# A mega-kernel's schedule table: output projection in four uses of bank 7, row preparation respread over the slots

## The chip, the cores and the metric

The kernel runs on one core of a Trainium2 chip. The metric is the device time of one execution in microseconds, median of several runs; the engines are TensorE (PE; its weight loads are PEld), VectorE (DVE), ScalarE (ACT), GpSimd (POOL) and SyncE (SP), which issues the DMAs.

## The reference

A layer with hyperbolic (Poincare) attention of 16 heads of width 16 over 8 sequences of 1024 tokens, and an FFN with one FP8-quantised product. Cut to what matters:

```python
x = x + attn(layernorm(x));  x = x + ffn(layernorm(x))
# attn, per head, c = softplus(log_c):
q_h, k_h, v_h = (exp_map_at_origin(split_heads(x @ W.T), c) for W in (W_q, W_k, W_v))
dist = poincare_distance(q_h, k_h, c)                 # arccosh(1 + 2c|q-k|^2 / ((1-c|q|^2)(1-c|k|^2)))
weights = softmax(-beta_pos * dist - attention_bias)
out_tan = einsum('bhst,bhtd->bhsd', weights, log_map_at_origin(v_h, c))
out = log_map_at_origin(exp_map_at_origin(out_tan, c), c)   -> concat @ W_o.T
# ffn: y = (e4m3(x / s_in) @ e4m3(kernel / s_k)) * (s_in * s_k), bf16, + bias
```

The exponential map needs a norm of each head's vector (an inverse square root, made here by a guess and three Newton steps on VectorE) and a tanh (made from one small exponential on ScalarE).

## The kernel before

The main loop has N = 512 steps: 16 stages (STEPS = 32 slots each) of 512 query tokens; in a stage, four groups of four heads, and for each group eight tiles of 128 keys. A slot s of stage G is one tile: distances of four heads by TensorE (`distances`, L1100, 18 x 128 weights on 512 columns, into banks 0 to 5), a logarithm of 128 x 2048 (`log`, L1217) and a power (`power`, L1224) by ScalarE, and the weighted values (`values`, L1115, summed in bank 6). The distances of slot n + 1 need the banks that the logarithm of slot n has read. In a unit of four slots whose flag says "open", VectorE bounds and clamps first (`bound` L1285, `clamp` L1294) and ScalarE reads its result (L1212); here three units of 128 are open: slots 4 to 7 of stage 5, 20 to 23 of stage 8, 12 to 15 of stage 15.

Beside this loop run the stages before and after the attention, all through the one bank 7, in *uses*: TensorE fills the bank, VectorE copies it out, and the next use waits for that copy. `project_stage` makes q, k, v of block n: X0 and X1 (transposes of the normalised input), M0 to M7 (the projections), R0 to R7 (transposes of the scaled rows of q and k), A0 and A1 (their largest entries, for the flags). `finish_stage` ends block n: T0, T1 (transposes), W (output projection, L695, and the residual, L723), Q0, Y0, Y1 (the FFN). S0 to S3 turn the sums of a head group (slots 2, 10, 18, 26; `turn_sums` L1124, `normalise` L1308 to L1312). The order is written out by hand: PROJECT_USES, FINISH_USES, FIRST_USES (project 1) and SECOND_USES (project 2) name slot and half for each use. From project 3 on, table slot k lies in slot k - 4 of stage n - 2; the finish of block n has k = slot in stage n + 1. BOTH means that the first half of the use goes ahead of the slot's values on TensorE and the second half behind them; a use with half 0 or 1 is done whole there. Slots without a use get two filler matmuls (`keep_busy`, L1138), except the slot BARE.

The functions `vector` of both stages hold VectorE's other work by table slot k: squares and sums (L587, L588), guess and Newton steps (L261 to L269), nrm (L596), the scaling of v (L598 to L604), the tanh and the row entries (L610 to L629), and `scale_rows` (L554). ScalarE's small exponential (`scalar`, L529) waits for nrm. In each slot VectorE first makes the copies of that slot's uses, in order (`copy`), then `copy_sums`, then the finish's and the project's other work. Before a unit of four slots each engine waits for a flag, loads it and branches. `Steps` makes VectorE wait for an own result where the next instruction reads it: a call waits, `mark` doesn't. In stage 15 SHORT_SLOTS says which table slots of the finish of block 14 fall into which slot. Ahead of the loop, project 0 and most of project 1 are done in many banks (FIRST_FILLS), and behind it comes the finish of block 15 (`last_tensor`, `last_vector`) with fillers at L1142.

## Time and profile before

| | |
|---|---|
| median of 3 runs | 1991.97 us (1991.16 to 1992.04) |
| the profiled execution | 1994.49 us, span 1992.7 us |
| mean granted TensorE clock | 0.972 of full speed |
| ScalarE busy | 1869.9 us, 94% |
| TensorE busy | 1788.6 us, 90% |
| VectorE busy | 1142.9 us, 57% |
| loop | first logarithm at 47.3, last power over at 1955.9 us |

A row of the trace gives start, duration, engine, line, operation, output and inputs and, in brackets, how long the engine was idle before and what released it. Consecutive instructions of one line stand in one row (x8: eight records, two for each fp32 matmul). Durations overlap a little on one engine, so the pitch from start to start is what counts. "DVEq" is VectorE's sequencer; "issue" is idle time for which the profile shows no wait.

### The profile page before, as it was taken

How to read it: one execution, taken by the hardware profiler on the slowest of the kernel's cores; microseconds unless marked ns; L12 is line 12 of the kernel's file. 1: busy time of each engine (PE TensorE's matmuls, PEld its weight loads, DVE VectorE, ACT ScalarE, POOL GpSimd, SP SyncE). 2: the span in 40 equal slices, each digit the busy share in tenths (PEclk: the TensorE clock that was granted, in tenths of full speed). 3: DMA queues.
4: the chain of work that ended last, by engine and by line, in shares of the span. 5: the costliest groups of instructions: out<-in, count | busy, mean ns of one | idle time of the engine just before them, and what ended most of it. 6: DMA issues, size and time to landing. Idle time of an engine off the chain costs nothing.

```text
span 1992.7 us, 29554 instructions
## 1 busy us (share of the span) xinstructions
PE 1788.6 (90%) x10713; PEld 603.1 (30%) x10713; DVE 1142.9 (57%) x2825; ACT 1869.9 (94%) x1094; POOL 12.8 (1%) x35
## 2 busy tenths in 40 slices
PE   7988989989898798989998898998989899899897
PEld 4322222323232232322322223232322223233234
DVE  7454565655656656565656647565565656323436
ACT  4889999999999799999998999999999999999883
POOL 2000000000000000000000000000000000000000
PEclk9799999999999899999999899999999999999889
DMA  1314213141312213132040321314131131411110
GB/s 56 112 49 144 54 54 103 42 134 43 112 44 78 77 44 112 43 101 75 23 134 22 110 67 44 112 43 134 40 107 52 56 90 43 123 43 53 33 33 23
DMA packets 112953, 142.54 MB, mean 72 GB/s; under 512 B 35691, under 2 KB 61548, under 8 KB 112748
## 3 DMA queue, kind: packets, MB, share of 16 engines
q1 hardware_dynamic: 112748, 140.13, 22.6%
q8 instruction: 89, 1.46, 0.3%
q14 instruction: 116, 0.95, 0.2%
HBM read 85.07 MB, written 55.05 MB: 70 GB/s over the span
## 4 chain that ended last, share of the span: by engine, by line
ACT 54%; PE 24%; issue 14%; DVE 4%; ACTq 3%; DMA 0%; DVEq 0%; SPq 0%
ACT U L1217 28%; ACT U L1224 26%; PE ps L1100 8%; PE ps L401 6%; PE ps L1115 5%; ACTq L1265 2%; PE ps L695 2%; DVE U L1294 1%; PE ps L1138 1%; PE ps L406 1%; PE ps L1142 1%; DVE U L1285 1%; DVE rows L554 0%; DMA U<-in_L_attn_W_o_dram 0%; ACT e L529 0%
## 5 line engine op out<-in xcount | busy, mean ns | idle before, releaser
L1224 ACT ACTIVATE U<-U 128x2048 f32<-128x2048 f32 x512 | 997.1, 1949 | 0.3
L1217 ACT ACTIVATE U<-ps 128x2048 f32<-128x2048 f32 x500 | 955.7, 1911 | 35.5 <-PE ps L1100 31.6
L1100 PE MATMUL ps<-q_T,k_T 18*128 18x512 f32 x4096 | 632.5, 652 | 133.0 <-ACT U L1217 107.7
L1115 PE MATMUL ps<-U,vals 128*32 128x512 f32 x4096 | 560.4, 620 | 29.4 <-ACT U L1224 28.9
L1100 PEld LDWEIGHTS ps<-q_T,k_T 18*128 18x128 f32 x4096 | 195.9, 187 | 356.8 <-ACT U L1217 296.4
L401 PE MATMUL ps<-wT,xnT 128*128 128x384 f32 x512 | 232.0, 545 | 4.9 <-DVEq L1318 2.5
L490 DVE COPY qkv<-ps 128x384 f32<-128x384 f32 x112 | 62.4, 557 | 243.7 <-PE ps L401 243.6
L1115 PEld LDWEIGHTS ps<-U,vals 128*32 128x32 f32 x4096 | 81.7, 109 | 205.4 <-ACT U L1224 159.2
L401 PEld LDWEIGHTS ps<-wT,xnT 128*128 128x128 f32 x512 | 81.1, 194 | 197.0 <-issue 132.4
L1138 PE MATMUL ps<-woT,ident 128*128 128x256 f32 x340 | 121.8, 441 | 3.8 <-DVEq L1318 3.6
L406 PE MATMUL ps<-ident,rows 128*128 128x128 f32 x512 | 107.2, 308 | 4.9 <-DVE rows L554 2.4
L406 PEld LDWEIGHTS ps<-ident,rows 128*128 128x128 f32 x512 | 55.1, 146 | 176.4 <-issue 114.5
L1138 PEld LDWEIGHTS ps<-woT,ident 128*128 128x128 f32 x340 | 52.0, 193 | 145.2 <-issue 116.0
L1300 DVE COPY OTs<-ps 128x512 f32<-128x512 f32 x64 | 43.8, 684 | 88.0 <-PE ps L1115 75.3
L498 DVE COPY q_T<-ps 128x512 f32<-128x512 f32 x60 | 41.5, 691 | 90.9 <-PE ps L406 90.3
L500 DVE COPY k_T<-ps 128x512 f32<-128x512 f32 x60 | 41.5, 691 | 62.8 <-PE ps L406 60.8
L695 PE MATMUL ps<-woT,fi_ocT 128*128 128x256 f32 x240 | 68.6, 409 | 0.0
L1308 DVE TENSOR_REDUCE den<-ps 128x16 f32<-128x256 f32 x64 | 27.2, 424 | 58.2 <-PE ps L1124 57.2
L695 PEld LDWEIGHTS ps<-woT,fi_ocT 128*128 128x128 f32 x240 | 41.0, 191 | 51.8 <-issue 37.3
L723 DVE TENSOR_TENSOR fi_x<-fi_xt,ps 128x512 f32<-128x512 f32 x30 | 20.6, 688 | 61.9 <-PE ps L695 61.9
L587 DVE TENSOR_TENSOR sqr<-qkv 128x768 f32<-128x768 f32 x56 | 53.3, 953 | 2.4
L588 DVE TENSOR_REDUCE ss<-sqr 128x48 f32<-128x768 f32 x56 | 53.4, 953 | 1.9
(209 smaller groups left out, 1179.6 us busy)
## 6 DMA issues: line engine op xcount, KB each, us to landing
rqb<-q_scratch SPq DMA_DIRECT2D x64, 1024.0 KB, 5.6
q_scratch<-q_T SPq DMA_DIRECT2D x16, 1024.0 KB, 4.5
k_scratch<-k_T SPq DMA_DIRECT2D x16, 1024.0 KB, 6.8
v_scratch<-vals SPq DMA_DIRECT2D x16, 768.0 KB, 9.6
...
```

What stands on the lines that cost most here:

```text
L401: ins = pe.matmul(bank[:, 0:384], xnT[:, dc, t * P:(t + 1) * P], g.wT[:, dc, half * 384:(half + 1) * 384], start=dc == 0, stop=dc == 1)
L406: ins = pe.transpose(bank[:, t * P:(t + 1) * P], rows[:, qk, t, hg * HPG:(hg + 1) * HPG, :].rearrange("p h r -> p (h r)"), g.ident[:, :])
L490: v.tensor_copy(qkv[:, t, 24 * half:24 * (half + 1), :].rearrange("p h d -> p (h d)"), bank[:, 0:384]).then_inc(a.b7_copied, 1)
L587: step(v.tensor_tensor(sqr[:, :], src, src, ALU.mult))
L588: step(v.tensor_reduce(ss[:, t, :], sqr[:, :].rearrange("p (h d) -> p h d", d=DH), AX.X, ALU.add))
L695: ins = pe.matmul(bank[:, a * D:(a + 1) * D], ocT[:, dc, t * P:(t + 1) * P], g.woT[:, dc, :], start=dc == 0, stop=dc == 1)
L1100: ins = pe.matmul(g.ps[:, 2 * pair + i, :], a.k_T[HB * h:HB * h + RD, b % 2, hg, kt * P:(kt + 1) * P], a.q_T[HB * h:HB * h + RD, G % 3, hg ...
L1115: ins = pe.matmul(g.ps[HB * h:HB * h + VW, 6, :], a.vals[:, b % 2, kt, (hg * HPG + h) // 2, DH * (h % 2):DH * (h % 2) + VW], U[:, n % RING ...
L1138: pe.matmul(g.ps[:, 7, 0:D], g.ident[:, :], g.woT[:, 0, :], start=True, stop=True)
L1217: act.activation(U[:, n % RING].rearrange("p b n -> p (b n)"), chunk(n), ACT.Ln, scale=-2.0 / EPS, bias=1.0).then_inc(freed, 1)
L1224: act.activation(U[:, n % RING], U[:, n % RING], ACT.Exp, scale=exponent).then_inc(exp_done, 1)
L1300: v.tensor_copy(OTs[:, :], g.ps[:, 6, :]).then_inc(ot_done, 1)
```

## The change

The tables: W becomes four uses (W0 to W3 in table slots 15, 16, 17, 19), each of one token tile with its bn_stats in the same slot; M3 goes from table slot 10 to 11; A0 from 27 to 24 (second half, alone in its slot); R2 is a use of both halves; the bare slot is 6. Project 2's and project 1's uses are moved likewise. VectorE's work: squares of tiles 1 and 2 from table slots 11 and 14 to 12 and 15, two Newton steps in slot 18 and one with nrm in 19, the scaling of v from 20 to 35, the tanh spread over 21 to 23, amax ahead of the second reciprocal, the row entries and the scaling of q's rows together in 24 (behind A0's copy), that of k's rows in 25. The small exponential moves from table slot 21 to 20, which is slot 16. The four stores go from 34 to 36. The finish has its first scaling in 7, the aggregates in 20, the last sum in 33. Stage 15 packs the finish of block 14 into earlier slots, and the tail has 19 fillers for 24. The rest of the diff renames slots accordingly.

```diff
@@ -47,32 +47,35 @@
...
-PROJECT_SLOTS = 35
-FINISH_SLOTS = 34
+PROJECT_SLOTS = 37
+FINISH_SLOTS = 35
 PROJECT_USES = {("X", 0): (4, BOTH), ("X", 1): (5, BOTH),
-                ("M", 0): (7, BOTH), ("M", 1): (8, BOTH), ("M", 2): (9, BOTH), ("M", 3): (10, BOTH),
+                ("M", 0): (7, BOTH), ("M", 1): (8, BOTH), ("M", 2): (9, BOTH), ("M", 3): (11, BOTH),
                 ("M", 4): (12, BOTH), ("M", 5): (13, BOTH), ("M", 6): (15, BOTH), ("M", 7): (16, BOTH),
-                ("R", 0): (25, BOTH), ("R", 1): (26, BOTH), ("R", 2): (27, 0), ("A", 0): (27, 1),
+                ("A", 0): (24, 1), ("R", 0): (25, BOTH), ("R", 1): (26, BOTH), ("R", 2): (27, BOTH),
                 ("R", 3): (28, BOTH), ("R", 4): (29, BOTH), ("R", 5): (31, 0), ("A", 1): (31, 1),
                 ("R", 6): (32, BOTH), ("R", 7): (33, BOTH)}
 TOLD = 12
-FINISH_USES = {("T", 0): (13, BOTH), ("T", 1): (14, BOTH), ("W", 0): (15, BOTH), ("W", 1): (17, BOTH),
+FINISH_USES = {("T", 0): (13, BOTH), ("T", 1): (14, BOTH), ("W", 0): (15, BOTH), ("W", 1): (16, BOTH),
+               ("W", 2): (17, BOTH), ("W", 3): (19, BOTH),
                ("Q", 0): (30, BOTH), ("Y", 0): (31, 0), ("Y", 1): (31, 1)}
-
-SHORT_USES = dict(FINISH_USES)
-SHORT_USES.update({("Q", 0): (28, BOTH), ("Y", 0): (30, 0), ("Y", 1): (30, 1)})
-BARE = 7
-SHORT_SLOTS = {23: (23, 24), 24: (25, 26), 25: (27, 28), 26: (29,), 27: (30, 31), 28: (32,), 29: (33,), 30: (), 31: ()}
+BARE = (6,)
+
+SHORT_SLOTS = {8: (8, 9, 10, 11, 12), 9: (13,), 10: (), 11: (14,), 12: (15,), 13: (16,), 14: (17, 18), 15: (19,), 16: (20, 21),
+               17: (22,),
+               18: (23,), 19: (24,), 20: (25,), 21: (26, 27), 22: (28, 29, 30), 23: (31, 32), 24: (33,), 25: (34,),
+               26: (), 27: (), 28: (), 29: (), 30: (), 31: ()}
 SUM_STEPS = 10
 
 
 FIRST_USES = {("A", 0): (2, 0), ("R", 4): (2, 0), ("A", 1): (2, 0), ("R", 5): (3, BOTH), ("R", 6): (6, BOTH),
-              ("R", 7): (11, BOTH), ("R", 0): (14, BOTH), ("R", 1): (17, BOTH), ("R", 2): (19, BOTH),
-              ("R", 3): (20, BOTH)}
+              ("R", 7): (14, BOTH), ("R", 0): (17, BOTH), ("R", 1): (19, BOTH), ("R", 2): (20, BOTH),
+              ("R", 3): (21, BOTH)}
 
 SECOND_USES = dict(PROJECT_USES)
-SECOND_USES.update({("R", 0): (25, BOTH), ("R", 1): (26, BOTH), ("R", 2): (27, 0), ("A", 0): (27, 1), ("R", 3): (28, 0),
-                    ("R", 4): (28, 1), ("R", 5): (29, BOTH), ("R", 6): (30, 0), ("A", 1): (30, 1), ("R", 7): (31, BOTH)})
+SECOND_USES.update({("M", 2): (9, BOTH), ("M", 3): (11, BOTH),
+                    ("R", 0): (25, BOTH), ("R", 1): (27, 0), ("R", 2): (27, 1), ("R", 3): (28, 0), ("R", 4): (28, 1),
+                    ("R", 5): (29, BOTH), ("R", 6): (30, 0), ("A", 1): (30, 1), ("R", 7): (31, BOTH)})
 
 FIRST_FILLS = ([("X", 0, 0, 6), ("X", 0, 1, 7)] + [("M", 0, i, (2, 3, 4, 5, 6, 7, 2, 3)[i]) for i in range(8)]
...
+    OWN = {0: 9, 1: 10, 9: 2, 12: 2, 15: 2, 17: 3, 18: 7, 19: 3, 21: 2, 22: 4, 23: 5, 24: 4}
     PER = sum(OWN.values())
 
...
+        if k == 36:
             b, u = n // 2, n % 2
...
+                pe.wait_ge(rows_rdy, 2 * n + (1 + i // HG if n >= 2 else 2 - i // HG))
         ins = fill(pe, n, key, g.ps[:, 7, :], part)
         if part != 0:
...
 
     def scalar(act, n, k):
-        if k == 21:
+        if k == 20:
             act.wait_ge(n_rdy, n + 1)
...
             ins.then_inc(xn_rdy, 1)
-        if k in (9, 11, 14, 17):
-            t = {9: 0, 11: 1, 14: 2, 17: 3}[k]
+        if k in (9, 12, 15, 17):
+            t = {9: 0, 12: 1, 15: 2, 17: 3}[k]
             v.wait_ge(a.b7_copied, uses.after(("M", n, 2 * t + 1)))
...
             root_guess(v, step, ss[:, :, :], y[:, :, :])
+            newton(v, step, ss[:, :, :], y[:, :, :], y2[:, :, :], 2)
+        if k == 19:
             newton(v, step, ss[:, :, :], y[:, :, :], y2[:, :, :], 1)
-        if k == 19:
-            newton(v, step, ss[:, :, :], y[:, :, :], y2[:, :, :], 2)
             v.tensor_tensor(nrm[:, :, :], ssqk, yqk, ALU.mult).then_inc(n_rdy, 1)
-        if k == 20:
+        if k == (31 if n == 2 else 35):
+            step = first or Steps(v, g_steps, 2 * (n - 2))
             step(v.tensor_scalar(vg[:, :, :], y[:, :, 2 * H:], g.ZS, 1.0, ALU.mult, ALU.min))
...
             step(v.reciprocal(rp[:, :, :], rp[:, :, :]))
+        if k == 22:
             step.mark(v.tensor_scalar(tn[:, :, :], e[:, :, :], -1.0, 1.0, ALU.mult, ALU.add))
             step(v.tensor_tensor(a4[:, :, :], e[:, :, :], rp[:, :, :], ALU.mult))
             step.mark(v.tensor_tensor(tn[:, :, :], tn[:, :, :], rp[:, :, :], ALU.mult))
             step(v.tensor_tensor(a4[:, :, :], a4[:, :, :], rp[:, :, :], ALU.mult))
-        if k == 22:
+        if k == 23:
+            step.mark(v.tensor_scalar(a4[:, :, :], a4[:, :, :], 4.0, A_FLOOR, ALU.mult, ALU.max))
             step.mark(v.tensor_tensor(tt[:, :, :], tn[:, :, :], tn[:, :, :], ALU.mult))
             step.mark(v.tensor_tensor(f[:, :, 0:H], tn[:, :, 0:H], yqk[:, :, 0:H], ALU.mult))
-            step.mark(v.scalar_tensor_tensor(f[:, :, H:], tn[:, :, H:], 2.0, yqk[:, :, H:], ALU.mult, ALU.mult))
-            step(v.tensor_scalar(a4[:, :, :], a4[:, :, :], 4.0, A_FLOOR, ALU.mult, ALU.max))
+            step(v.scalar_tensor_tensor(f[:, :, H:], tn[:, :, H:], 2.0, yqk[:, :, H:], ALU.mult, ALU.mult))
+            v.tensor_reduce(amax[:, :], a4[:, :, :].rearrange("p t h -> p h t"), AX.X, ALU.max).then_inc(amax_rdy, 1)
             step(v.reciprocal(rp[:, :, :], a4[:, :, :]))
-        if k == 23:
+        if k == 24:
             if n >= 4:
                 v.wait_ge(a.stored, 64 * n)
             step.mark(v.tensor_copy(rows[:, 0, :, :, 17], tt[:, :, 0:H]))
             step.mark(v.tensor_copy(rows[:, 0, :, :, 18], rp[:, :, 0:H]))
             step.mark(v.tensor_copy(a.rk[:, b % 2, :, u * GT:(u + 1) * GT], rp[:, :, H:].rearrange("p t h -> p h t")))
             step.mark(v.tensor_scalar(rows[:, 1, :, :, 16], tt[:, :, H:], -1.0, None, ALU.mult))
-            v.tensor_reduce(amax[:, :], a4[:, :, :].rearrange("p t h -> p h t"), AX.X, ALU.max).then_inc(amax_rdy, 1)
-        if k == 24:
-            scale_rows(v, n, (1, 0))
-        assert first or step.n == OWN.get(k, 0), (k, step.n)
+            if n >= 2:
+                scale_rows(v, n, (0,))
+        if k == 25:
+            scale_rows(v, n, (1,))
...
-                sp.wait_ge(steps_v, PER * (n - 1) + sum(count for slot, count in OWN.items() if slot <= 28))
+                sp.wait_ge(steps_v, PER * (n - 1) + sum(count for slot, count in OWN.items() if slot <= 27))
             sp.dma_start(xt[:, :, :], g.x_g[n]).then_inc(f_in, 16)
-        if k == 33:
+        if k == 34:
             sp.wait_ge(res_rdy, n + 1)
...
-            for a in halves(part, range(2)):
-                t = 2 * i + a
-                for dc in range(2):
-                    ins = pe.matmul(bank[:, a * D:(a + 1) * D], ocT[:, dc, t * P:(t + 1) * P],
-                                    g.woT[:, dc, :], start=dc == 0, stop=dc == 1)
+            for dc in halves(part, range(2)):
+                ins = pe.matmul(bank[:, 0:D], ocT[:, dc, i * P:(i + 1) * P], g.woT[:, dc, :],
+                                start=dc == 0, stop=dc == 1)
         elif kind == "Q":
...
                     v.wait_ge(res_out, 16 * n)
-            v.tensor_tensor(x1[:, two, :].rearrange("p t d -> p (t d)"),
-                            xt[:, two, :].rearrange("p t d -> p (t d)"), bank, ALU.add).then_inc(b7_copied, 1)
+            v.tensor_tensor(x1[:, i, :], xt[:, i, :], bank[:, 0:D], ALU.add).then_inc(b7_copied, 1)
         elif kind == "Q":
...
                             y[:, :, :].rearrange("p t h -> p (t h)").unsqueeze(2).broadcast_to([P, GT * H, DH]),
                             ALU.mult).then_inc(oc_rdy, 1)
-        if k == 21:
-            v.wait_ge(b7_copied, uses.after(("W", n, 1)))
-            for t in range(GT):
-                step.mark(v.bn_stats(stats[:, t, :], x1[:, t, :]))
+        if k in (15, 16, 17, 19):
+            t = {15: 0, 16: 1, 17: 2, 19: 3}[k]
+            v.wait_ge(b7_copied, uses.after(("W", n, t)))
+            step.mark(v.bn_stats(stats[:, t, :], x1[:, t, :]))
+        if k == 20:
             step.settle()
...
         if k == 26:
             v.tensor_tensor(xq[:, :, :].rearrange("p t d -> p (t d)"), sp2, sp1, ALU.subtract).then_inc(xq_rdy, 1)
-        if k == 28:
+        if k == 27:
             step(v.tensor_reduce(rmax[:, :], xt[:, :, :], AX.X, ALU.max, apply_absolute_value=True))
...
         pe.wait_ge(l_act, 2)
-        keep_busy(1, 24)
+        keep_busy(1, 19)
...
                         use(*key, 0)
-                    unused = n > 2 and s != BARE and not in_step(G, s, 0) + in_step(G, s, 1)
+                    unused = n > 2 and s not in BARE and not in_step(G, s, 0) + in_step(G, s, 1)
```

## Rows read from the trace of the kernel before

**Rows 1.** The page's first section, and one row of the waits.

```profile
PE 1788.6 (90%) x10713; PEld 603.1 (30%) x10713; DVE 1142.9 (57%) x2825; ACT 1869.9 (94%) x1094; POOL 12.8 (1%) x35
...
ACT U L1217 <- PE ps L1100: 31.6, 21, 5.9
```

**Rows 2.** Timeline of ScalarE, stage 9, slots 16 to 20 (start, duration).

```profile
1192.16 1.88 ACT L1217 ACTIVATE U<-ps 128x2048 f32<-128x2048 f32 x1
...
1195.99 1.88 ACT L1217 ACTIVATE U<-ps 128x2048 f32<-128x2048 f32 x1
...
1199.56 0.39 ACT L529 ACTIVATE e<-nrm,sc 128x128 f32<-128x128 f32 x1
1199.85 1.87 ACT L1217 ACTIVATE U<-ps 128x2048 f32<-128x2048 f32 x1
...
1207.07 1.87 ACT L1217 ACTIVATE U<-ps 128x2048 f32<-128x2048 f32 x1
```

**Rows 3.** Timeline of TensorE, stage 9: slot 15, and slot 21's first transpose.

```profile
1190.52 1.24 PE L1100 MATMUL ps<-q_T,k_T 18*128 18x512 f32 x8 [0.33 <-ACT U L1217]
1191.69 1.13 PE L695 MATMUL ps<-woT,fi_ocT 128*128 128x256 f32 x4
1192.75 1.07 PE L1115 MATMUL ps<-U,vals 128*32 128x512 f32 x8
1193.75 1.13 PE L695 MATMUL ps<-woT,fi_ocT 128*128 128x256 f32 x4
...
1213.73 0.44 PE L406 MATMUL ps<-ident,rows 128*128 128x128 f32 x2
```

**Rows 4.** Timeline of VectorE, stage 9, slots 15 to 20.

```profile
1197.54 0.36 DVE L269 SCALAR_TENSOR_TENSOR y<-y 128x192 f32<-128x192 f32 x1
1197.93 0.29 DVE L596 TENSOR_TENSOR nrm<-ss,y 128x128 f32<-128x128 f32 x1
1199.34 0.69 DVE L1300 COPY OTs<-ps 128x512 f32<-128x512 f32 x1 [1.12 <-issue]
...
1207.71 0.95 DVE L621 RECIPROCAL rp<-a 128x128 f32<-128x128 f32 x1
...
1209.14 0.37 DVE L629 TENSOR_REDUCE amax<-a 128x32 f32<-128x128 f32 x1
1210.04 2.36 DVE L554 TENSOR_TENSOR rows<-qkv,f 128x1024 f32<-128x1024 f32 x2 [0.53 <-issue]
```

**Rows 5.** VectorE's groups by form: count, busy, mean ns, idle before.

```profile
L752 DVE BATCH_NORM_STATS2 fi_stats<-fi_x 128x6 f32<-128x256 f32 x60 | 20.9, 412 | 2.7 <-issue 2.7
...
L502 DVE TENSOR_REDUCE amax_r<-ps 32x1 f32<-32x128 f32 x16 | 4.5, 278 | 8.6 <-PE ps L411 8.6
...
L886 DVE TENSOR_TENSOR fi_x<-fi_xt,ps 128x256 f32<-128x256 f32 x4 | 1.7, 417 | 0.7 <-PE ps L842 0.7
```

**Rows 6.** First stage: ScalarE and TensorE rows; then stretches (length, busy, PEclk last but two).

```profile
109.50 1.88 ACT L1217 ACTIVATE U<-ps 128x2048 f32<-128x2048 f32 x1 [5.93 <-PE ps L1100]
...
68.09 2.09 PE L1100 MATMUL ps<-q_T,k_T 18*128 18x512 f32 x8
...
73.22 2.09 PE L1100 MATMUL ps<-q_T,k_T 18*128 18x512 f32 x8
...
165.75 0.44 PE L406 MATMUL ps<-ident,rows 128*128 128x128 f32 x2 [1.72 <-DVEq L1318]
...
160.00:166.70 6.70, 4.38 (x34) 1.65 (x34) 2.65 (x7) 6.66 (x4) 0.00 (x0) 1.00 0.01 0
166.70:173.50 6.80, 6.80 (x35) 2.02 (x31) 1.46 (x3) 3.78 (x3) 0.00 (x0) 0.50 0.01 2
```

**Rows 7.** Timeline of ScalarE, stage 8, slot 20: first logarithm of the open unit.

```profile
1085.72 1.91 ACT L1212 ACTIVATE U<-U 128x2048 f32<-128x2048 f32 x1 [4.65 <-DVE U L1294]
```

**Rows 8.** The tail: TensorE's fillers, and VectorE's last step ahead of the transposes.

```profile
1969.26 10.63 PE L1142 MATMUL ps<-woT,ident 128*128 128x256 f32 x48
...
1977.67 1.23 DVE L903 TENSOR_TENSOR fi_xq<-fi_ocT,fi_osq 128x1024 bf16<-128x1024 f32 x1
```

45 lines of the change are left out of this document (20 added, 25 removed).

## Prediction

> **What bounds the kernel now.** I read the shares first: ScalarE is busy for 94% of the span, TensorE for 90%, VectorE for 57% [rows 1]. The waits of ScalarE before its logarithm come second: 31.6 us of idle time behind the distances, in only 21 places [rows 1]. So the rhythm is ScalarE's, one logarithm and one power per slot, and time is lost in a few places. Third comes the timeline of a regular stage, stage 9. I count from the start of the logarithm of slot 16, at 1192.16. A logarithm starts 3.57 us before the place where the next could start: slot 17's at 1195.99, and its successor's place is taken at 1199.56 by the small exponential, which pushes the next logarithm to 1199.85, 0.29 later [rows 2]. I use 3.56 for a full ScalarE slot. From slot 16 to slot 20 the logarithms need 1207.07 - 1192.16 = 14.91 instead of 14.24, so 0.67 is lost per stage: 0.29 to the small exponential, 0.38 to the doubled output projection in slots 15 and 17, which makes TensorE late [rows 2, 3]. What slots 5 to 8 lose to the projections of q, k, v stays (below).
>
> TensorE's order in a slot is fixed: distances (first at 1.92 after its logarithm), first half of a use, the values as soon as the power is over, second half [rows 3]. VectorE runs its own program in order: a copy out of bank 7 waits for the second half, and all that stands behind that copy waits too.
>
> **Part 1, the output projection in four uses, and the exponential in slot 16.** A whole use is now one quarter: a half takes 0.53 instead of 1.06 [rows 3]. TensorE is no longer late in slots 15 to 19 and 0.38 goes. But in slot 15 VectorE must copy the first quarter, do bn_stats, three Newton steps and the product nrm, and the small exponential in slot 16 waits for nrm. Slot 15 starts at 1188.60 (1192.16 less 3.56): distances at 1190.52, values at 3.72, so at 1192.3, second half from 1193.31, filled at 1193.9, copied from 1194.0, that is 1.86 after slot 16's logarithm. Then 0.42 for a copy of 256 columns plus 0.04, 0.33 for bn_stats (four take 1.4, mean 0.41, overlapping) [rows 5], 3 x 0.39, and 0.29 for nrm [rows 4]: 4.11. The exponential starts at 4.15 instead of 3.56, the next logarithm at 4.44. Slots 16 to 20 then take 4.44 + 3 x 3.56 = 15.12, against 14.91: **+0.21 per stage**, x 13 stages = +2.7. In stage 14, without projections, only the 0.38 is gained: -0.4. What hid nrm before was a whole slot between it and the exponential.
>
> **Part 2, rows and A0.** This is the part that decides. Before, slot 19 had no use of bank 7, VectorE ran ahead, and both scalings of the rows started at 1210.04, 2.97 after slot 20's logarithm at 1207.07, and were over at 5.33; the first transpose R0 was due at 1213.73, that is 6.66 [rows 2, 3, 4]. Now slot 19 holds the last quarter (W3) and slot 20 holds A0, and the whole chain stands behind them. From slot 20's logarithm: W3 is copied from 1.85 (as above) to 2.31; bn_stats to 2.64; the four small products before the reciprocal at 1207.71, 0.73 as there; amax 0.28 (its 0.37 less the overlap); the reciprocal 0.95 and its wait: 4.64 [rows 4]. Slot 20 begins a unit of four, where the sequencer waits for that reciprocal, reads the flag and branches: the same gap was 1.12 of issue at 1199.34 [rows 4], I take 1.05: 5.7. A0's reduction 0.28 [rows 5] and two semaphores: 6.15. The aggregates that the finish stage now has in slot 20, 0.6: 6.75. The four copies, 0.44 up to 1209.14, and the wait for the stores: 7.25. The q scaling, half of 2.36 [rows 4]: **rows ready at 8.5, due at 6.66**. TensorE stands for 1.85 us, with the values queued behind R0. R0's halves and the values take 0.37 + 0.99 + 0.37, so the next distances come at 10.3 instead of 9.05, and the logarithm of slot 23 at 11.46 instead of 10.68: +0.78 even if nothing else happens.
>
> The clock is what else happens. In the first stage TensorE stood 1.72 before a row transpose (165.75); over 160 to 166.7 it was busy 4.38 of 6.70, and from 166.7 to 173.5 the granted clock was 0.50, the 1.2 GHz level; ScalarE was then busy only 3.78 of 6.80 [rows 6]. The new gap of 1.85 follows a slot with no fillers (A0 replaces both), with gaps of 0.5 on each side of its values. Between 5.05 and 8.5 TensorE would work 1.24, less than in the case above. I expect the fall in nearly each stage. At the low level a slot with a row transpose takes 73.22 - 68.09 = 5.13 [rows 6] instead of 3.56; two such slots, the second logarithm about 2.1 after its distances begin, put slot 24's logarithm at 10.3 + 5.13 + 2.1 = 17.5 instead of 14.24: **+3.3**. Bounds: 1.8 if the clock comes back within a slot, 4.5 by the first stage's case with its stall (1.72 + 3.0 of ScalarE idle, rounded). It meets stages 1 to 13 except 8, where slots 20 to 23 are an open unit: 12 x 3.3 = +40 (22 to 54).
>
> The Trainium skill's page "TensorE: Matmul & The Clock Gate", section "HAM oscillation — how this bites in real kernels", ties the fall to waits long enough to cross an idle stretch, longer than this gap. By that rule the clock would hold here and 12 x 0.78 would be all (rival A). This case's trace disagrees with so mild a reading: it fell after a gap of 1.72 [rows 6].
>
> **Part 3, the open unit of stage 8.** Its first logarithm waited 4.65 us for VectorE's clamp [rows 7]. VectorE enters the unit after slot 19's work: before at about 17.9 after slot 16's logarithm (1210.04 - 1192.16), now at 15.12 + 5.7 = 20.8: +2.9.
>
> **Part 4, first stage.** M3 leaves the slot of the sums, where its wait ended in 5.93 us of idle ScalarE [rows 6], and R1 leaves slot 26, worth about 4. Against it: the squares of tile 1, two long instructions, now stand ahead of the quantising of the FFN kernel in slot 12, so M5's copy and R7 behind it come over 2 us late, a gap of the kind that cost 5.93; and slot 25 waits 1.2 for its rows. Between -10 and +2; I take -5.
>
> **Part 5, last stage and tail.** The finish of stage 14 runs up to four slots earlier. That empties slots 25 to 29, but puts T1's copy ahead of the open unit at slots 12 to 15 (+3.7 by the same count as part 3) and quarters into it. I take +0.8, between -5 and +6. In the tail five of 24 fillers go. They run from 1969.26 for 10.63, VectorE delivers xq at 1978.90 [rows 8], so at most 0.9 is open, and copies that wait for other work follow: -0.3.
>
> **At nothing**, each with its cover: M3 one slot later and the bare slot 6 for 7 (three projections in a row each side of the bare slot instead of four and two: the same lateness by the count of matmuls, an estimate); squares two slots later (VectorE idles there); Newton steps in slot 14 (2.4 us before the first quarter is filled, 0.4 to spare); v scaling to slot 31 (1.9 us, behind Y1's copy, 0.6 to spare); the four stores two slots later on SP's queue, whose first reader loads them a stage later.
>
> **The sum**, against the profiled execution (1994.49, its span 1992.7 and 1.8 around it): +2.7 - 0.4 + 40 + 2.9 - 5 + 0.8 - 0.3 = +40.7, so 2035.2. The median of the runs shown is 2.5 lower: **2033**. With 22 to 54 for part 2 and +-6 for the rest the forecast's own range is 2010 to 2052.
>
> **Rivals.** A, the rows are late but the clock holds: 12 x 0.78 = 9.4 instead of 40: 2002. For it: W3's and R0's matmuls lie around the gap. B, the change works: VectorE makes both appointments. The point is 4.8 us from W3's copy to the rows; I count 6.65. Then 13 x -0.38, -0.4, first stage -5, -0.3, no part 3: -10.6, that is 1981, faster. For it: VectorE has 43% idle, and my prices of semaphores and the branch could be too high, though hardly by 1.8. C, the gap of slot 16 (TensorE idle 1.06 while ScalarE waits for nrm) lowers the clock too: 13 x 2 more, 2059. D, it all cancels within 0.2%.
>
> **How the numbers follow.** About 0.2% (4 us) is what a measurement of this kernel can tell from no change. Forecast 0.60, A 0.17, B 0.12, C 0.07, D 0.04. Slower: 0.60 + 0.17 + 0.07 = 0.84, less a little of A: 0.83; faster 0.11; same 0.06. The range leaves out B and half of C: 1999 to 2056.
>
> **What would show it.** In the changed profile: L529's exponential in slot 16 with about 0.6 idle before it, released by nrm; the first row transpose of slots 21 with 1.5 to 2 us idle, released by the scaling of the rows, in each of stages 1 to 13; the granted clock at 0.5 for some slots behind it, mean clock well under 0.972; slots 15 to 19 without a late distance. If R0 starts without a gap, part 2 is wrong and the time is near 1981; if the gap is there and the clock stays 1.0, it is near 2002.

## The result and the profile after

The changed kernel takes 2038.51 us (median of 6 runs, 2036.11 to 2044.67) against 1992.01 for the kernel before (6 runs, 1991.16 to 1994.11): a ratio of 1.0235, 95% interval 1.0218 to 1.0252. The forecast was 2033, range 1999 to 2056. The profiled execution of after took 2036.56, its span is 2034.8, 42.1 more than before's, and its mean granted clock is 0.954 instead of 0.972. It lies 1.95 below the median of its kernel, where the forecast took 2.5 above; against the profiled execution the forecast was 2035.2.

First the page: the shares, and the groups of the logarithm and of the rows' transposes (busy, mean ns | idle before).

```profile
PE 1781.0 (88%) x10523; PEld 577.6 (28%) x10523; DVE 1145.2 (56%) x2855; ACT 1871.5 (92%) x1094; POOL 12.6 (1%) x35
...
L1218 ACT ACTIVATE U<-ps 128x2048 f32<-128x2048 f32 x500 | 954.9, 1910 | 60.0 <-PE ps L1101 57.5
...
L409 PE MATMUL ps<-ident,rows 128*128 128x128 f32 x512 | 117.9, 328 | 32.8 <-DVE rows L556 29.9
```

The engines have nearly the work of [rows 1]: VectorE is busy for 2.3 us more, ScalarE for 1.6 more, TensorE for 7.6 less. ScalarE waits 57.5 us for distances instead of 31.6, and TensorE waits 29.9 us for the scaling of the rows, where it waited 2.4 us in the kernel before. The two are one thing, as stage 9 shows. ScalarE there, from slot 16 (answers to [rows 2]):

```profile
1220.22 1.87 ACT L1218 ACTIVATE U<-ps 128x2048 f32<-128x2048 f32 x1
...
1224.46 0.40 ACT L532 ACTIVATE e<-nrm,sc 128x128 f32<-128x128 f32 x1 [0.56 <-DVE nrm L598]
1224.77 1.86 ACT L1218 ACTIVATE U<-ps 128x2048 f32<-128x2048 f32 x1
...
1235.44 1.88 ACT L1218 ACTIVATE U<-ps 128x2048 f32<-128x2048 f32 x1
...
1249.00 1.88 ACT L1218 ACTIVATE U<-ps 128x2048 f32<-128x2048 f32 x1 [2.75 <-PE ps L1101]
1250.77 1.90 ACT L1225 ACTIVATE U<-U 128x2048 f32<-128x2048 f32 x1
1253.33 1.88 ACT L1218 ACTIVATE U<-ps 128x2048 f32<-128x2048 f32 x1 [0.66 <-PE ps L1101]
```

The exponential waits 0.56 for nrm. The logarithms of slots 23 and 24 wait 2.75 and 0.66 for distances. TensorE in the same stage (answers to [rows 3]):

```profile
1226.68 1.24 PE L1101 MATMUL ps<-q_T,k_T 18*128 18x512 f32 x8 [1.03 <-ACT U L1218]
...
1239.17 1.07 PE L1116 MATMUL ps<-U,vals 128*32 128x512 f32 x8 [0.56 <-ACT U L1225]
1240.17 0.28 PE L414 MATMUL ps<-ident,amax 128*32 128x128 f32 x1
1240.94 1.24 PE L1101 MATMUL ps<-q_T,k_T 18*128 18x512 f32 x8 [0.48 <-ACT U L1218]
1244.59 0.41 PE L409 MATMUL ps<-ident,rows 128*128 128x128 f32 x2 [2.41 <-DVE rows L556]
...
1246.87 2.09 PE L1101 MATMUL ps<-q_T,k_T 18*128 18x512 f32 x8
```

TensorE stands 2.41 before R0, and the distances behind it take 2.09 instead of 1.24. VectorE is the releaser (answers to [rows 4]):

```profile
1237.41 0.42 DVE L727 TENSOR_TENSOR fi_x<-fi_xt,ps 128x256 f32<-128x256 f32 x1 [2.50 <-PE ps L699]
...
1239.21 0.94 DVE L626 RECIPROCAL rp<-a 128x128 f32<-128x128 f32 x1
1241.74 0.28 DVE L505 TENSOR_REDUCE amax_r<-ps 32x1 f32<-32x128 f32 x1 [1.58 <-issue]
1242.16 0.38 DVE L759 BATCH_NORM_AGGREGATE fi_mv<-fi_stats 128x2 f32<-128x6 f32 x4
...
1243.22 1.22 DVE L556 TENSOR_TENSOR rows<-qkv,f 128x1024 f32<-128x1024 f32 x1
```

W3's copy waits 2.50 for TensorE, then the chain runs through the unit's edge (1.58), A0's reduction, the aggregates and the copies. The clock, in stretches of one slot from 1241.58 (length, busy of PE, PEld, DVE, ACT, POOL, then PEclk):

```profile
1241.58:1245.14 3.56, 1.15 (x14) 0.36 (x10) 2.48 (x11) 3.56 (x3) 0.00 (x0) 1.00 0.52 194
1245.14:1248.70 3.56, 3.56 (x18) 0.81 (x10) 1.72 (x2) 1.11 (x1) 0.00 (x0) 0.55 0.42 103
1248.70:1252.26 3.56, 3.56 (x20) 1.04 (x20) 0.26 (x2) 3.26 (x2) 0.00 (x0) 0.50 0.02 5
```

TensorE is at its 1.2 GHz level for nearly two slots, full all the time, and in the first of them ScalarE is busy for 1.11 of 3.56 us. It is not so in every stage. Stage 11, the stretch behind such a gap, R0, and the logarithm of slot 23:

```profile
1483.00:1486.50 3.50, 3.50 (x28) 0.87 (x20) 1.82 (x2) 2.61 (x2) 0.00 (x0) 1.00 0.40 109
```
```profile
1482.49 0.41 PE L409 MATMUL ps<-ident,rows 128*128 128x128 f32 x2 [2.08 <-DVE rows L556]
...
1485.37 1.88 ACT L1218 ACTIVATE U<-ps 128x2048 f32<-128x2048 f32 x1 [0.89 <-PE ps L1101]
```

The clock held, and the whole stall costs 0.89 of idle ScalarE. Of the twelve regular stages (1 to 13 without 8) the clock held in two, 1 and 11, and fell in ten.

To put a number on each part I took the time from each logarithm to the next, less 3.56, and added it up by stage and slot. The excess goes to the later of the two slots. In all it is 84.0 us before and 126.6 after. The differences:

| part | before | after | difference |
|---|---|---|---|
| slots 16 to 19, stages 1 to 13 | 8.7 | 12.7 | +4.0 |
| slots 20 to 27, twelve regular stages | 0 | 41.5 | +41.5 |
| stage 8 from slot 20 on | 12.8 | 14.4 | +1.6 |
| stage 5, slots 0 to 15 | 16.0 | 18.5 | +2.5 |
| other slots 0 to 15, stages 1 to 13 | 6.9 | 6.5 | -0.5 |
| first stage | 24.0 | 21.0 | -3.0 |
| stage 14 | 0.8 | -0.1 | -0.9 |
| last stage | 14.9 | 12.2 | -2.7 |

### The profile page after: what moved, and what is told of

Read it like the earlier page. It is cut to its first block, busy times and chain, and to the rows that moved or that the text cites. A ratio compares the mean times of both kernels' runs of the same rounds, so it can differ in the third digit from the quotient of the medians.

```text
span 2034.8 us, 29206 instructions
## 1 busy us (share of the span) xinstructions
PE 1781.0 (88%) x10523; PEld 577.6 (28%) x10523; DVE 1145.2 (56%) x2855; ACT 1871.5 (92%) x1094; POOL 12.6 (1%) x35
## 4 chain that ended last, share of the span: by engine, by line
ACT 43%; PE 33%; issue 12%; DVE 9%; ACTq 2%; DVEq 1%; DMA 0%; SPq 0%
ACT U L1218 24%; ACT U L1225 19%; PE ps L1101 12%; PE ps L1116 9%; PE ps L404 8%; PE ps L409 2%; ACTq L1266 2%; PE ps L699 2%; DVE U L1295 1%; DVE rows L556 1%; DVE rp L626 1%; DVE U L1286 1%; DVE fi_x L727 1%; DVE fi_stats L755 1%; DVEq L1365 0%
## 5 line engine op out<-in xcount | busy, mean ns | idle before, releaser
L1218 ACT ACTIVATE U<-ps 128x2048 f32<-128x2048 f32 x500 | 954.9, 1910 | 60.0 <-PE ps L1101 57.5
L1225 ACT ACTIVATE U<-U 128x2048 f32<-128x2048 f32 x512 | 996.3, 1948 | 0.3
L1101 PE MATMUL ps<-q_T,k_T 18*128 18x512 f32 x4096 | 650.0, 666 | 162.8 <-ACT U L1218 124.9
L1116 PE MATMUL ps<-U,vals 128*32 128x512 f32 x4096 | 573.1, 633 | 32.5 <-ACT U L1225 31.6
L1101 PEld LDWEIGHTS ps<-q_T,k_T 18*128 18x128 f32 x4096 | 202.3, 191 | 390.3 <-ACT U L1218 322.5
L409 PE MATMUL ps<-ident,rows 128*128 128x128 f32 x512 | 117.9, 328 | 32.8 <-DVE rows L556 29.9
L409 PEld LDWEIGHTS ps<-ident,rows 128*128 128x128 f32 x512 | 57.5, 154 | 242.6 <-issue 183.2
L501 DVE COPY q_T<-ps 128x512 f32<-128x512 f32 x60 | 41.5, 691 | 114.1 <-PE ps L409 114.1
L727 DVE TENSOR_TENSOR fi_x<-fi_xt,ps 128x256 f32<-128x256 f32 x60 | 25.3, 421 | 116.6 <-PE ps L699 116.6
L699 PE MATMUL ps<-woT,fi_ocT 128*128 128x256 f32 x240 | 86.2, 441 | 0.0
L503 DVE COPY k_T<-ps 128x512 f32<-128x512 f32 x60 | 41.5, 692 | 50.5 <-PE ps L409 48.9
L699 PEld LDWEIGHTS ps<-woT,fi_ocT 128*128 128x128 f32 x240 | 36.7, 193 | 99.8 <-issue 77.0
L1213 ACT ACTIVATE U<-U 128x2048 f32<-128x2048 f32 x12 | 22.9, 1911 | 37.3 <-DVE U L1295 37.3
L1139 PE MATMUL ps<-woT,ident 128*128 128x256 f32 x160 | 56.2, 434 | 0.0
L721 DVE COPY fi_ocT<-ps 128x512 f32<-128x512 f32 x30 | 20.7, 692 | 57.4 <-PE ps L695 57.4
```

Of the source, the lines that this page charges most:

```text
L409: ins = pe.transpose(bank[:, t * P:(t + 1) * P], rows[:, qk, t, hg * HPG:(hg + 1) * HPG, :].rearrange("p h r -> p (h r)"), g.ident[:, :])
L699: ins = pe.matmul(bank[:, 0:D], ocT[:, dc, i * P:(i + 1) * P], g.woT[:, dc, :], start=dc == 0, stop=dc == 1)
L727: v.tensor_tensor(x1[:, i, :], xt[:, i, :], bank[:, 0:D], ALU.add).then_inc(b7_copied, 1)
L1101: ins = pe.matmul(g.ps[:, 2 * pair + i, :], a.k_T[HB * h:HB * h + RD, b % 2, hg, kt * P:(kt + 1) * P], a.q_T[HB * h:HB * h + RD, G % 3, hg ...
L1116: ins = pe.matmul(g.ps[HB * h:HB * h + VW, 6, :], a.vals[:, b % 2, kt, (hg * HPG + h) // 2, DH * (h % 2):DH * (h % 2) + VW], U[:, n % RING ...
L1139: pe.matmul(g.ps[:, 7, 0:D], g.ident[:, :], g.woT[:, 0, :], start=True, stop=True)
```

## The experiments

The theory: R0 comes late because VectorE's chain stands behind W3 and A0; the stall alone costs about 1 us a stage, and the fall of the clock that it brings costs two to three times as much again. Rivals: the clock only accompanies a loss that the wait makes; or A0, or W3, or the wait of slot 16 alone is the cause. Every kernel was timed beside the kernel before on the same chip, and ratios are to that. An expectation of so many us stands against 2038.5 for the change and 1992.0 for before, so 2011 is a ratio of 1.0096.

**The clock taken away, the wait kept.** In slot 21 of stages 1 to 13 TensorE gets fillers ahead of R0.

```diff
+                    if s == 21 and 1 <= G < LAST - 1:
+                        pe.wait_ge(a.b7_copied, first_use[n])
+                        keep_busy_again(7, 10)
                     for key in both:
                         use(*key, 0)
```

With ten:

> The changed kernel with ten fillers (128x256 matmuls whose result nobody reads) on TensorE in slot 21 of stages 1 to 13, behind the distances and ahead of the wait for the rows. They fill 10 x 0.22 of the 2.1 to 2.4 us in which TensorE stood; the rows come as late as before. My theory: the stall costs 1.02 a stage, as stages 1 and 11 of the changed kernel show, and the fall of the clock the rest, 2.84 to 4.47 in all in each of ten stages (39.5 together). With TensorE kept busy the clock holds in all twelve: 39.5 - 10 x 1.02 = 29.3 less, 2009. Rival, the clock is only a companion and the time is the stall's and VectorE's: no change or a little slower, 2038 to 2042. Second rival, the fall is prompted by something else in the slot (the DMA traffic, the light matmuls of A0): the clock still falls, 2038.

Measured: 1.0276 (1.0245 to 1.0306), so slower still. Stage 9:

```profile
1246.28 4.58 PE L1143 MATMUL ps<-woT,ident 128*128 128x256 f32 x20
1250.70 0.38 PE L409 MATMUL ps<-ident,rows 128*128 128x128 f32 x2
```

The number was missed for a plain reason, and the row shows it: ten fillers are x20 in the trace and take 4.58, so one is 0.46. I had read [rows 8] as 48 fillers in 10.63, where it is 24. TensorE was thus busy past the moment when the rows were ready, and R0 came at 11.11 after slot 20's logarithm. What the run did tell is clean: the clock held in all twelve stages at this place, and each was late by 3.25 to 3.33. With stage 11 of the change (R0 at 8.82, 1.02 late) this gives the point from which a late R0 costs, 7.8 after slot 20's logarithm, and behind it one us costs one us.

With five:

> As the kernel with ten fillers, but with five. In that kernel each filler took 0.46 us, not the 0.22 that I had counted (ten took 4.58), so that R0 came at 11.11 after slot 20's logarithm instead of 8.81 to 9.15, and slot 23's logarithm 3.27 late in every one of the twelve stages; the clock held in all twelve at the rows' place. The two place the point from which a late R0 costs anything at 11.11 - 3.27 = 7.84 and 8.81 - 1.02 = 7.79. Five fillers take 2.3, as long as TensorE stood. My theory: R0 starts when it did, at 8.8 to 9.15, each stage is 1.0 to 1.35 late, the clock holds: 2038.5 - 41.5 + 12 x 1.2 = 2011. Rival, what is lost is the stall's and the clock is a companion: 2036 to 2040.

Measured: 1.0119 (1.0088 to 1.0151), 2011.08 against the 2011 expected. The median of before was 1987.9 beside it, so the equal times are in part luck: by the ratio it lies 0.2% above the expected 1.0096, which is within the interval. Stage 9:

```profile
1229.15 0.41 PE L409 MATMUL ps<-ident,rows 128*128 128x128 f32 x2
...
1232.04 1.88 ACT L1221 ACTIVATE U<-ps 128x2048 f32<-128x2048 f32 x1 [1.21 <-PE ps L1101]
```

Nothing was made earlier here: 65 matmuls that nobody reads were added, and the rows are as late as in the change. Each regular stage is late by 1.11 to 1.39 (14.7 in all), the clock falls at this place in none, and half of the whole loss is gone. So the clock is a cause of its own and no companion. Of the 41.5 us some 12 to 15 are the stall and the rest, about twice that, is the clock.

**The wait made harmless.** R0 goes whole behind the values:

```diff
-                ("A", 0): (24, 1), ("R", 0): (25, BOTH), ("R", 1): (26, BOTH), ("R", 2): (27, BOTH),
+                ("A", 0): (24, 1), ("R", 0): (25, 1), ("R", 1): (26, BOTH), ("R", 2): (27, BOTH),
```

> The changed kernel with one appointment moved: R0, the first transpose of the rows, runs whole in the second half of slot 21, behind the values, instead of half before and half behind them. VectorE's chain is as it was and the rows are as late, 9.05 after slot 20's logarithm. My theory: the values (due at 7.28) no longer queue behind R0, the gap of 2.4 becomes 0.56 and about 0.9, R0 is over at 9.95 and the distances follow 0.9 late instead of 1.5, so slot 23's logarithm is late by about 0.45 instead of 1.02, and the clock holds: 2038.5 - 41.5 + 12 x 0.45 = 2002. If the clock falls in spite of the split gap: 2025 to 2035. Rival, only the moment when the rows are ready counts: no change, 2038.

Measured: 1.0051 (1.0031 to 1.0071), as expected (1.005). The same entry is changed for project 2. VectorE's chain is untouched. The values no longer queue behind R0:

```profile
1216.88 1.06 PE L1116 MATMUL ps<-U,vals 128*32 128x512 f32 x8 [0.56 <-ACT U L1225]
1218.73 0.63 PE L409 MATMUL ps<-ident,rows 128*128 128x128 f32 x4 [0.79 <-DVE rows L556]
```

The pause of 2.41 became 0.56 and 0.79, the clock fell at this place in none of twelve stages, and slot 23 is 0 to 0.25 late where 0.45 was expected. Slots 20 to 27 of the regular stages lose 1.0 instead of 41.5, so this one move gives back nearly all that part 2 lost. That the ratio hit all the same is luck: slots 16 to 19 lost 15.6 instead of 12.7, as the clock fell after the pause of slot 16 in three stages, and the first stage 16.0 instead of 21.0.

**Who makes the rows late.** A0 back in slot 23, in the half where it was:

```diff
-                ("A", 0): (24, 1), ("R", 0): (25, BOTH), ("R", 1): (26, BOTH), ("R", 2): (27, BOTH),
+                ("R", 0): (25, BOTH), ("R", 1): (26, BOTH), ("R", 2): (27, 0), ("A", 0): (27, 1),
```

> The changed kernel with A0, the transpose of the maxima, back in its old place in slot 23 (and R2 beside it); W3 stays in slot 19 and the rows are scaled as in the changed kernel. My theory: both W3 and A0 delay the rows. From slot 20's logarithm the reciprocal ends at 4.7, the pause at the unit's edge 1.1, then 2.3 for aggregates, copies and the scaling of q: rows at 8.1 instead of 9.05, R0 due at 6.74, so TensorE stands 1.35 instead of 2.1 to 2.4 and the logarithm of slot 23 is late by about 0.1 instead of 1.02. If the clock holds in all stages: 2038.5 - 41.5 + 1.2 = 1998. If it falls in half of them all the same: 2016. Rival, W3's copy is the cause and A0 costs nothing: the gap stays over 2 us, 2036 to 2039. Rival, A0 is the whole cause: no gap, 1997.

Measured: 1.0158 (1.0134 to 1.0181), nearest to the branch "falls in half of them" (2016), whose ratio of 1.012 lies outside the interval. W3 alone leaves R0 a pause of 1.65 in five stages and 1.94 to 2.03 in seven, where I had 1.35. Stage 6:

```profile
872.72 0.41 PE L409 MATMUL ps<-ident,rows 128*128 128x128 f32 x2 [1.66 <-DVE rows L556]
```

The clock held in all five stages with 1.65 and fell in five of the seven others. Slots 20 to 27 lose 23.0 instead of 41.5: W3 alone makes the rows late, and A0 adds 0.4 us to it.

W3 away from slot 19, to slot 18, with A0 left in slot 20; then with the exponential back too; then with A0 back as well:

```diff
-               ("W", 2): (17, BOTH), ("W", 3): (19, BOTH),
+               ("W", 2): (17, BOTH), ("W", 3): (18, BOTH),
```

> The changed kernel with W3, the last quarter of the output projection, in slot 18 beside the transpose of the sums, instead of in slot 19; A0 stays in slot 20 and the exponential in slot 16. (The last group has its quarters one slot apart to match.) My theory: VectorE is then 3.56 us earlier with the reciprocal, and A0 alone sets the rows: A0 filled at 5.0 after slot 20's logarithm, reduced by 5.3, then 2.4 for aggregates, copies and the scaling: R0 at about 8.0 to 8.2, 0.2 to 0.4 beyond the point where it costs. TensorE stands 1.4, and with A0 taken out the clock fell in none of the five stages whose gap was 1.65, in five of seven at 1.94 to 2.03. So no falls: 2038.5 - 41.5 + 3.6, and stage 8's open unit is entered 3.3 earlier, and slot 18 is 0.1 late 13 times: 1998.6. Rival, A0 is the cause and W3 is innocent: R0 as late as before, 2036. Rival, three uses of TensorE in slot 18 do not fit (1.24 + 0.66 + 1.4 + 1.07 = 4.4, less overlaps): 0.5 in each of 13 stages more, 2005.

> W3 in slot 18 and the small exponential in slot 17; A0 stays in slot 20. By my theory the two effects are separate and add: 1998.6 less 13 x 0.7 = 1989.5, a little under the kernel before. If the wait of slot 16 was hidden behind something else: 1998.

> The changed kernel with all three suspects undone: W3 in slot 18, the small exponential in slot 17, A0 in slot 23. The quarters of the output projection, the new places of M3 and of the first stage and the earlier finish of the last group stay. By my theory R0 of slot 21 starts without a gap, no clock falls there, the exponential costs 0.29 and slots 15 and 17 are not late: 2038.5 - 41.5 - 9.1 - 3.3 + 1.3 = 1986, 0.3% faster than the kernel before. If A0 in slot 23 makes slots 23 to 25 late as it did not in the kernel before, or the open unit of stage 8 stays late: 1990, no difference. A rival: W3 in slot 18 keeps VectorE so long that slot 18 to 20 run late: over 1995.

Measured: 1.0371 (1.0341 to 1.0402), 1.0356 (1.0315 to 1.0396) and 1.0270 (1.0244 to 1.0295). All three missed, and for one reason that none of my rivals named. Stage 9 of the first, TensorE and the end of VectorE's steps on the sums:

```profile
1245.49 0.66 PE L1125 MATMUL ps<-ident,OTs 128*128 128x128 f32 x4
1248.00 0.70 PE L699 MATMUL ps<-woT,fi_ocT 128*128 128x256 f32 x2 [1.84 <-DVEq L1319]
```
```profile
1247.40 0.49 DVE L1313 TENSOR_TENSOR on<-ps,den 128x128 f32<-128x128 f32 x2
```

Slot 18 turns the sums in bank 7, and bank 7 is free only when VectorE has taken them; W3's first half waits 1.84 for that, with the values behind it. I had counted TensorE's matmuls and not the bank's round trip through VectorE. In the third kernel the exponential's 0.29 and this pause (1.79) are all that is left in slots 16 to 27 of the regular stages: slot 20's logarithm is 1.87 late in the three stages where the clock held, 3.5 to 3.9 in the nine where it fell, and slot 21's up to 1.3 more. So they make the same pair of costs, a pause and a fall, in another slot and behind another step of VectorE. The second and the third differ by A0 and R2 alone, and with A0 in slot 20, W3 out of its way, R0 waits for the rows again. Stage 5 of the second:

```profile
758.58 0.41 PE L409 MATMUL ps<-ident,rows 128*128 128x128 f32 x2 [1.16 <-DVE rows L556]
```

This pause is 0.89 to 1.18 in its twelve regular stages, the clock fell at it in six of them, and slots 20 to 27 lose 69.1. With A0 back in slot 23 the pause is gone, and they lose 46.2. So A0 alone makes the rows late too.

**All undone that hurt, the rest kept.** The last two quarters share slot 17, one in each half, the exponential is in slot 17, A0 in slot 23:

```diff
-               ("W", 2): (17, BOTH), ("W", 3): (19, BOTH),
+               ("W", 2): (17, 0), ("W", 3): (17, 1),
...
-        if k == 20:
+        if k == 21:
             act.wait_ge(n_rdy, n + 1)
```

> The last two quarters of the output projection both in slot 17: W2 whole ahead of the values, W3 whole behind them. The small exponential is in slot 17, A0 in slot 23. With W3 in slot 18 TensorE stood 1.8 us in every stage, since the slot of the sums leaves no room for a second use of bank 7: the use waits for VectorE's four steps on the sums. In slot 17 nothing of that kind stands in the way. My theory: slot 17 has the matmuls that a doubled slot had before, 0.19 late (the doubled slot 15 is single now); the exponential costs 0.29; R0 of slot 21 has no gap, no clock falls in a regular stage, stage 8's open unit is entered as early as before. Per stage 0.48 instead of 0.67: -2.5; first stage -3 and last stage -2.6 as the changed kernel had them: 1984 against 1992 for the kernel before, a ratio of 0.996. Rival, the moved appointments of the first stage and of the last group gain only by the luck of the clock there: ratio 0.9985. Rival, W3's copy between W2's and the sums makes the sums late: over 1.00.

Measured: 0.9962 (0.9947 to 0.9977), where 0.996 was expected: faster than both kernels. The sum hit, its terms did not. In the profiled execution slots 16 to 19 lose 5.0 less than before (2.5 less expected), the first stage 6.7 less (3) and the last stage 3.9 less (2.6), while stage 5 loses 3.9 more and stage 14 3.6 more, which wasn't counted at all. R0 in slot 21 of stage 9 has no wait ahead of it:

```profile
1205.54 1.24 PE L1100 MATMUL ps<-q_T,k_T 18*128 18x512 f32 x8
1206.71 0.44 PE L409 MATMUL ps<-ident,rows 128*128 128x128 f32 x2
1207.34 1.07 PE L1115 MATMUL ps<-U,vals 128*32 128x512 f32 x8 [0.19 <-ACT U L1224]
```

The same with the FFN kernel's quantising in slot 10 of the first stage (`KERNEL_STEP = 10`):

> The same, and VectorE quantises the FFN kernel in slot 10 of the first stage, where its long steps stand behind the sums' and ahead of M3's copy, instead of in slot 12. In the changed kernel the pair of squares and these steps held M5's copy until 116.24, and R7 waited for it 2.36 us: slot 16's logarithm was 1.68 late. In slot 10 TensorE has no other use, M3's copy comes 1.2 late and M4's first half 0.7. My theory: 1.2 to 1.6 us less than with slot 12, a ratio lower by 0.0007; the clock of the first stage, which falls in other places in other runs, can move this by 3 us either way. Rival: nothing, because the stall moves to slot 11.

Measured: 0.9954 (0.9935 to 0.9973). R7's pause is gone; of slot 16's 1.67 us, 0.96 came back in slot 14. The two intervals overlap, so this gain isn't shown.

From the faster kernel each suspect was then put back alone. A0 in slot 20, with R2 in both halves as in the change:

> The kernel with W2 and W3 in slot 17 and the exponential in slot 17, but A0 in slot 20 as in the change: A0 alone. W3 no longer holds VectorE. My theory: A0 is filled at 5.0 after slot 20's logarithm, reduced by 5.3, and 2.3 to 2.4 more for the aggregates, the copies and the scaling of q: rows at 7.8 to 8.0, R0 0.1 to 0.3 beyond the point where it costs (7.8), TensorE stands 1.2 to 1.4, and the clock holds, as it did in all five stages with a gap of 1.65. 12 x 0.2 = 2.4 more: 0.9962 + 0.0012 = 0.9974. Rival, A0 was the whole cause and costs what it did in the changed kernel, 8.8 or more after slot 20's logarithm: 12 x 1.0 with the clock held, 1.002, or with falls up to 1.017.

Measured: 1.0069 (1.0042 to 1.0095), so +0.0107 where +0.0012 was expected. Stage 9, the reduction, then TensorE:

```profile
1227.56 0.28 DVE L505 TENSOR_REDUCE amax_r<-ps 32x1 f32<-32x128 f32 x1 [2.81 <-PE ps L414]
```
```profile
1227.24 0.29 PE L414 MATMUL ps<-ident,amax 128*32 128x128 f32 x1
1228.01 1.24 PE L1100 MATMUL ps<-q_T,k_T 18*128 18x512 f32 x8 [0.48 <-ACT U L1217]
1230.41 0.41 PE L409 MATMUL ps<-ident,rows 128*128 128x128 f32 x2 [1.16 <-DVE rows L556]
1230.75 1.93 PE L1115 MATMUL ps<-U,vals 128*32 128x512 f32 x8
```

The chain is as counted: R0 at 7.92 after slot 20's logarithm (1222.49), a pause of 1.16, and in the two stages where the clock held, 0.12 late. But the clock held in two stages only and fell in ten, with a shorter pause than the 1.65 that left it up five times. Ten may be more than is usual: the traced execution was the slowest of six, at a mean clock of 0.956 where the others had 0.958 to 0.967. In eight of the ten the clock fell before R0 started, by 0.03 to 0.65, that is inside the pause. The nearest difference between the two is slot 20: there fillers stood around the values, here A0's one matmul has their place and the pauses of 0.56 and 0.48 beside it. My expectation went by the length of the one pause and was wrong in that; that the thin slot 20 is the reason is argued and not shown. The kernel with R0 behind the values has the same thin slot 20 and pauses of 0.56 and 0.79, and never fell; what separates it from this one is not settled, and A0 in slot 20 with fillers beside it was not tried.

The exponential in slot 16:

> The kernel with W2 and W3 in slot 17 and A0 in slot 23, but the small exponential in slot 16 again: the one part alone, with no late rows behind it. My theory: 0.99 instead of 0.29 a stage as in the changed kernel, 13 x 0.70 = 9.1 more than the kernel with the exponential in slot 17: 0.9962 + 0.0046 = 1.0008 of the kernel before. Rival, TensorE's pause of 1.03 in slot 16 does lower the clock in some stages (the first trace of the exponential's removal could not exclude it, 10 falls of 12 against 9): 3 to 4 us for each, 1.003 or more. Rival, part of the wait lies under the doubled slot 17, so 0.5 a stage: 0.9995.

Measured: 1.0060 (1.0038 to 1.0082), +0.0098 where +0.0046 was expected. In the trace slot 17 is 0.99 late in each of 13 stages, as in the change, and slot 18 no longer 0.29; slot 19 loses 0.25 more, since the doubled slot 17 has no slack behind the pause; and in stages 5 and 13, where the clock fell after the pause of slot 16, slot 19 loses 1.84. Stage 5:

```profile
728.51 1.24 PE L1100 MATMUL ps<-q_T,k_T 18*128 18x512 f32 x8 [1.03 <-ACT U L1217]
729.68 1.83 PE L699 MATMUL ps<-woT,fi_ocT 128*128 128x256 f32 x4
```
```profile
730.00:733.40 3.40, 3.40 (x13) 0.97 (x11) 0.42 (x1) 3.40 (x3) 0.00 (x0) 0.50 0.00 0
```

Slots 16 to 19 of the 13 stages thus hold 19.2 instead of 3.7, that is 15.5 more for the 9.1 expected. In this execution the first and the last stage were 6.7 us longer besides and stage 14 4.0 shorter, which I can't tie to the edit.

The same part taken out of the change instead, with nothing else moved:

> The changed kernel with one part undone: the small exponential is back in slot 17 (the table's slot 21). Nothing else moves. My theory: in the changed kernel the logarithm of slot 17 comes 0.99 us late in each of 13 stages, 0.29 of it the exponential itself and the rest the wait for nrm and the pause that it leaves behind. Back in slot 17 the wait is hidden: 13 x 0.70 = 9.1 us less, 2029.4 against 2038.5. The rows of slot 21 stay as late as they were, and the clock still falls there. Rival 1, TensorE's pause of 1.03 us in slot 16 is what weakens it for the fall in slot 21: then falls in slot 21 vanish too, some 25 to 30 us more, about 2002. Rival 2, the 0.7 is taken from a slack that TensorE has later in the stage: no change, 2038.

Measured: 1.0152 (1.0131 to 1.0172), against 1.0188 expected. Slots 16 to 19 of the 13 stages fell from 12.7 to 3.7, which is the 9.0 expected. The rows' place lost 42.6 against 41.5, with nine falls instead of ten, so rival 1 (no falls left) is out. The median is 6.4 us below the profiled execution, which was the slowest of the four, at a clock of 0.950 where the others had 0.954 to 0.956: the part that the ratio gives beyond the 9.0 goes with that higher clock, but which falls were missing isn't known.

## Why the prediction was right

**The decisive step held: rows late, TensorE stands, the clock falls, in regular stages only.** The chain of part 2, counted from slot 20's logarithm at 1235.44: W3's copy at 1.97 (I had 1.85), the reciprocal over at 4.71 (4.64), A0's reduction over at 6.58 (6.15, as the edge took 1.58 where I took 1.05), rows ready at 9.00 (8.5), R0 at 9.15, pause 2.41 (1.85). The due time of 6.66 was 6.74. In the twelve regular stages the pause was 2.06 to 2.47, where the sign to look for was 1.5 to 2. Twelve times 3.3 made 40, the trace has 41.5. The runs with five fillers, with R0 behind the values and with the late uses moved away show each link of it.

**Two terms in it were off, and they cancel.** I had twelve falls at 3.3 each. There were ten, at 2.8 to 4.5, mean 3.95, and two stages at 1.0. The stall alone costs 1.0 (stages 1 and 11) to 1.39 (the run with five fillers), not 0.78, because the rows came at 8.7 to 9.1 instead of 8.5. So my certainty of a fall in each stage was too high and the price of one too low. My upper bound of 4.5 was set below the 4.7 that its own two numbers make, and the dearest stage took 4.47. All the other parts together were +0.7 by my count and +0.6 in the trace, though single ones missed by up to 3.5: that this sum came out is luck.

**Rival A was wrong in kind, not only in size.** By it the clock holds and 12 x 0.78 is all. The run with five fillers is that world made by hand. Rival A's 2002, with the stall at some 1.2 instead of 0.78, is 2007; measured were 2011, and by the ratio 2016. The Trainium skill's page "TensorE: Matmul & The Clock Gate", section "HAM oscillation — how this bites in real kernels", explains the fall by waits of some 3 to 5 us on a DMA between groups of matmuls. Here no single pause in the regular stages was longer than 2.47, the releaser was VectorE, and the clock fell in ten of twelve; the measurement decides. That section's picture, a fall paid again in each turn of the loop, is what the trace shows in ten of twelve stages.

**Rival C was half right.** The pause of 1.03 in slot 16 lowered the clock in none of 13 stages of the change, but in one to four of 13 in the other kernels that have it (A0 back 1, five fillers 1, R0 behind the values 3, ten fillers 4, the exponential put back into the faster kernel 2, W3 in slot 18 3). Each cost 0.9 to 1.0, 1.6 behind a doubled slot. Two us in each of 13 stages was far too much.

**Rival B, VectorE makes both appointments,** needed 4.8 us from W3's copy to the rows; it took 7.0 (1237.41 to 1244.44).

**Part 1.** The exponential started 4.24 after slot 16's logarithm (4.15 counted) and slots 16 to 20 took 15.22 (15.12). +4.0 instead of +2.7, 0.1 in each of 13 stages. Stage 14: -0.9 instead of -0.4.

**Part 3.** Stage 8's unit:

```profile
1115.44 1.91 ACT L1213 ACTIVATE U<-U 128x2048 f32<-128x2048 f32 x1 [7.95 <-DVE U L1295]
```

7.95 instead of 4.65 [rows 7], +3.3 for the 2.9 counted. The later slots of the unit gave half back, so +1.6 stayed. I had stopped at the first logarithm.

**Part 4.** -3.0 against -5. M3's 6.0 went, and R7's stall came where it was foretold, behind the quantising:

```profile
116.85 0.44 PE L409 MATMUL ps<-ident,rows 128*128 128x128 f32 x2 [2.36 <-DVE qkv L493]
```
```profile
119.76 1.88 ACT L1218 ACTIVATE U<-ps 128x2048 f32<-128x2048 f32 x1 [1.56 <-PE ps L1101]
```

The falls of the clock in slots 23 to 28 moved, but stayed. How much of the -3.0 the change made is open: with the same first stage, the traces with five fillers, with ten and with W3 in slot 18 have 17.7, 21.5 and 20.5 there, as the clock fell in other places.

**Part 5, the sign was wrong.** +0.8 counted, -2.7 measured. The step "puts T1's copy ahead of the open unit, +3.7" held:

```profile
1920.32 1.91 ACT L1213 ACTIVATE U<-U 128x2048 f32<-128x2048 f32 x1 [4.66 <-DVE U L1295]
```

It was 1.76 before, and the slot lost 7.0 instead of 3.7; slots 13 to 19 lose 2.6 more. The term that failed is what is emptied. Slots 27 to 29 gave 4.4, since the pause ahead of the last group's Q (2.09 in slot 26, with a fall behind it) is gone, and slots 9 to 11 gave another 4.1, which I had not counted at all. That second part is luck of the clock and no gain of the change. Before, the clock fell there behind two short pauses, and the change has the same two (0.56 and 0.70) without a fall:

```profile
1855.80 1.81 PE L1100 MATMUL ps<-q_T,k_T 18*128 18x512 f32 x8 [0.70 <-ACT U L1217]
...
1856.30:1866.60 10.30, 10.30 (x38) 2.43 (x30) 1.82 (x2) 7.58 (x5) 0.00 (x0) 0.50 0.01 2
```

With five fillers and in the two last kernels with W3 in slot 18 it fell there again. Without this 4.1 part 5 would be at +1.4, where I had counted +0.8. The tail gave 0.7 (0.3 counted, of at most 0.99 by [rows 8]).

**A step at nothing that wasn't.** The bare slot 6 for 7. In stage 5 the open unit ends with slot 7, at the low clock. Before, slot 7 had no projection and slot 8 began with TensorE idle for 0.97; now slot 7 has one, and slot 9's logarithm is 2.46 late (1.5 to 3.0 in the other kernels), +2.5 in all. My count of matmuls was of a regular stage, where it is right (-0.5), and the cover was a slot in one stage.
